# Second norm finished on VectorE and placed early in the step of a fused attention and mixture-of-experts layer

## The chip, the cores and the metric

One core of a Trainium2 chip runs the whole program. The metric is the device time in microseconds (us) of one execution. Three executions of the kernel before took 957.63, 956.96 and 951.90 us, median 956.96 us.

## The reference

For each of 8 batch rows of 1024 tokens with 256 features, the layer computes (cut to what matters; `mod` holds six vectors per row):

```
h = _layernorm(x) * (1 + ca) + sa
x = x + ga * _L0_attn_ref(h, W_in, W_out)   # Chebyshev features of q and k, 6 orders, 16 heads,
                                            # cumulative sums of k*v over the tokens, num / den
h = _layernorm(x) * (1 + cb) + sb           # the second norm
shared = silu(h @ sW1 + sb1) @ sW2 + sb2
activation = sqrt(softplus(h @ routing_W + bias)); the best 2 of 8 experts weigh
routed = sum_e cf[e] * (silu(h @ rW1[e] + rb1[e]) @ rW2[e] + rb2[e])
x = x + gb * (shared + routed)
```

All is float32. The second norm divides by sqrt(variance + 1e-5), over the 256 features of a token.

## The kernel before, in words

**Tiling.** A row is cut into two chunks of 512 tokens, p = 0 and p = 1. The program is a software pipeline over the 16 chunks. In the step (i, p) four chunks are worked on at once: chunk c+2 gets its first norm (ScalarE), chunk c+1 its q, k and v products, chunk c its attention, chunk c-1 its second norm, logits and routing weights, and chunk c-2 its nine experts (one shared, eight routed). The order of instructions on each engine is written out by hand in five functions `step`, one for each of TensorE, VectorE, ScalarE, GpSimd and the DMA queue of SyncE. Engines run their own lists strictly in order and meet only at semaphores. Steps (0,0) and (0,1) leave out what has no chunk yet, the last four leave out what has none any more; (7,1) has attention, second norm and experts, (8,0) second norm and experts, (8,1) experts alone.

**A step of TensorE (`step`, L1503).** Products of expert 0 and 1 into two PSUM banks that take turns (`ring`, L1368), the biases of the experts (L1476), transposes of the first norm (L1359), expert 0's second product (L1487), four of the six products for q and k, expert 1, transposes of the second norm, expert 2, the logits (L1394), sums over heads (L1421) with the transposed logits (L1402) between them, expert 3, v, expert 4, denominators (L1434), experts 5 to 8, then the projection `project_out` (L1445), which waits for VectorE's quotient `divide` (L1088), and last `combine_by_expert` (L1457, L1459), the transposes of the routing weights. A ring bank is filled again only once ScalarE has copied it out.

**The second norm before.** VectorE adds the projection to x (`residual`, L1096) and takes `bn_stats` (L378). GpSimd then works out mean and inverse deviation in ten small operations (`inv_std`, L353 to L366), and behind them in the same queue comes `weigh_order_5` (L653), a product of 128x1024 that VectorE's fifth prefix sum needs much later. ScalarE normalises the four token tiles (`normalise_second`, L435) in turn with its copies of q and k out of the ring (L800). TensorE transposes them, ScalarE scales the high parts (`highs`, L788), and VectorE makes the low parts (`lows(1)`, L968).

**The routing weights before.** `logit_parts` (L1107 to L1124), `exps` on GpSimd (L672), `softplus` (L1133 to L1150), `scores` on GpSimd (L681), `combine_weights` (L1158, L1162), seven small operations of `split_weights` on GpSimd (L698 to L703), `combine_by_expert` on TensorE, `combine_rows` on ScalarE (L860, L861), then DMAs that spread the rows over all partitions (`cfw`) for `weigh_hidden` (L1169), which VectorE does once for each of the eight experts.

**The quotient.** `invert` (L1072, L1074) on VectorE, a DMA to `inv_rows`, two that spread it back (L576, L581), `finish_numerator` (L1081), then `divide` (L1088). `output` (L1178) and two operations of `odd` for the next chunk (L984, L986) follow, and then `residual` of the next step.

## Time and profile before

| what | us |
|---|---|
| median of three executions | 956.96 |
| the profiled execution | 953.07 |
| its span, from first to last instruction | 951.3 |
| TensorE busy | 860.2 (90%) |
| VectorE busy | 815.7 (86%) |
| ScalarE busy | 489.8 (51%) |
| GpSimd busy | 408.3 (43%) |

The profiled execution lies 1.75 us above its span and 3.89 us below the median. Busy time of TensorE is that of pipelined matmuls and says nothing of how full the array is. In the middle of the program a row of the timeline is one instruction or a merged run of equal ones; what stands in brackets is the idle time of the engine before it and what ended that.

### The profile page before, as it was taken

The page shows a single profiled execution, that of the slowest core. Times are in us where ns is not written, and L with a number is a line of the kernel's source. Part 1 is how long each engine was busy: PE and PEld are TensorE (multiplying, and loading weights), DVE is VectorE, ACT ScalarE, POOL GpSimd, SP SyncE. Part 2 cuts the span into 40 slices and gives each one's busy share as a digit, 9 for nine tenths or more (in the row PEclk, how much of TensorE's full clock was granted, in tenths as well). Part 3 has the DMA queues.
Part 4 walks back from the last instruction along what each step waited for, and adds up shares of the span by engine and source line. Part 5 has one row for each costly group of instructions (what it writes and reads, how often), then busy time and mean ns, then how long its engine had stood idle before and what let it go on. Part 6 is the DMA issues. An engine that isn't in the chain of part 4 may idle for free. (4 is left out here: it accounts for less than half of the span.)

```text
span 951.3 us, 14272 instructions
## 1 busy us (share of the span) xinstructions
PE 860.2 (90%) x4377; PEld 648.6 (68%) x4377; DVE 815.7 (86%) x1263; ACT 489.8 (51%) x860; POOL 408.3 (43%) x502
## 2 busy tenths in 40 slices
PE   5766739999999999999999999999999999979998
PEld 4545427676767676786767676777767676756786
DVE  2696979999989998999989998999999998889423
ACT  4634546555556656655656566566556563441321
POOL 2341444363636355453636254543646253463220
PEclk9975769999999999999999999999999999999999
DMA  8014134453533535453534445354634243443422
GB/s 309 1 29 89 45 68 145 86 153 76 137 92 77 153 79 160 86 155 70 153 77 96 130 87 165 68 155 90 162 71 133 66 100 113 78 133 83 117 79 55
DMA packets 51705, 100.34 MB, mean 105 GB/s; under 512 B 5380, under 2 KB 34127, under 8 KB 49623
## 3 DMA queue, kind: packets, MB, share of 16 engines
q1 hardware_dynamic: 36356, 66.14, 21.2%
q0 software_dynamic: 14832, 33.03, 20.2%
q10 hardware_dynamic: 482, 0.74, 0.2%
q8 instruction: 18, 0.29, 0.1%
q14 instruction: 17, 0.13, 0.0%
HBM read 57.68 MB, written 17.06 MB: 79 GB/s over the span
## 5 line engine op out<-in xcount | busy, mean ns | idle before, releaser
L1487 PE MATMUL acc<-w,hid 128*128 128x256 f32 x1128 | 262.5, 380 | 2.6 <-DVE hid L1169 2.6
L1487 PEld LDWEIGHTS acc<-w,hid 128*128 128x128 f32 x1128 | 213.9, 190 | 37.6 <-DVE hid L1169 4.7
L845 ACT ACTIVATE hid<-ring,b1row 128x512 f32<-128x512 f32 x144 | 98.7, 685 | 143.0 <-PE ring L1368 140.4
L1169 DVE TENSOR_TENSOR hid<-hid,cfw 128x512 f32<-128x512 f32 x128 | 111.1, 870 | 37.0 <-DMA cfw<-cf_rows 21.6
L665 POOL DMA_DIRECT2D feat<-feat x48 | 43.7, 910 | 228.8 <-DVE feat L1046 115.0
L800 ACT ACTIVATE feat<-ring,bqkv 128x512 f32<-128x512 f32 x96 | 65.7, 686 | 81.9 <-PE ring L1368 81.9
L1368 PE MATMUL ring<-n2H,w1H 128*128 128x512 f32 x288 | 102.5, 437 | 0.0
L1445 PE MATMUL tr<-wo_g,feat 128*128 128x256 f32 x256 | 65.3, 413 | 35.9 <-DVE feat L1088 35.9
L1021 DVE TENSOR_TENSOR_SCAN feat<-zero,carry,feat 128x512 f32<-128x512 f32 x80 | 97.1, 1261 | 0.0
L1021 DVE TENSOR_TENSOR_SCAN feat<-zero,feat 128x512 f32<-128x512 f32 x80 | 95.7, 1243 | 0.0
L1368 PE MATMUL ring<-n2H,w1L 128*128 128x512 f32 x288 | 90.8, 397 | 0.0
L1368 PE MATMUL ring<-n2L,w1H 128*128 128x512 f32 x288 | 90.5, 395 | 0.0
L1421 PE MATMUL tr<-feat,const 128*32 128x512 f32 x640 | 89.1, 602 | 0.0
L1445 PEld LDWEIGHTS tr<-wo_g,feat 128*128 128x128 f32 x256 | 51.6, 207 | 49.2 <-DVE feat L1088 33.7
L1368 PE MATMUL ring<-n1H,winH 128*128 128x512 f32 x192 | 69.5, 444 | 15.2 <-issue 7.9
L820 ACT ACTIVATE feat<-feat,const 128x1024 f32<-128x1024 f32 x64 | 70.2, 1142 | 1.0
L353 POOL TENSOR_TENSOR ms<-stats 128x4 f32<-128x4 f32 x18 | 30.2, 1678 | 88.4 <-DVE stats L378 88.4
L1368 PEld LDWEIGHTS ring<-n2H,w1L 128*128 128x128 f32 x288 | 54.4, 189 | 12.7
L1368 PEld LDWEIGHTS ring<-n2L,w1H 128*128 128x128 f32 x288 | 54.5, 189 | 12.5
L1368 PE MATMUL ring<-n1H,winL 128*128 128x512 f32 x192 | 62.8, 409 | 0.0
L1368 PE MATMUL ring<-n1L,winH 128*128 128x512 f32 x192 | 62.8, 409 | 0.0
L1368 PEld LDWEIGHTS ring<-n2H,w1H 128*128 128x128 f32 x288 | 48.8, 191 | 18.5 <-issue 11.7
(171 smaller groups left out, 1559.8 us busy)
## 6 DMA issues: line engine op xcount, KB each, us to landing
feat<-feat POOLq DMA_DIRECT2D x48, 512.0 KB, 4.6
cfw<-cf_rows SPq DMA_DIRECT2D x16, 1280.0 KB, 7.6
xin<-in_L_attn_x SPq DMA_DIRECT2D x16, 512.0 KB, 9.3
feat<-inv_rows SPq DMA_DIRECT2D x32, 256.0 KB
cfw<-cf_rows SPq DMA_DIRECT2D x16, 512.0 KB, 3.6
out<-x SPq DMA_DIRECT2D x15, 512.0 KB, 8.5
out<-fin POOLq DMA_DIRECT2D x15, 512.0 KB, 6.0
cfw<-cf_rows SPq DMA_DIRECT2D x16, 256.0 KB, 4.5
```

The lines of the kernel that those rows point to most:

```text
L353: nc.gpsimd.tensor_tensor(t(1), m0, m1, ALU.subtract).then_inc(mv_steps[n], 1)
L665: g.dma_start(f(into), f(of), accum_op=ALU.add).then_inc(added[n], 16)
L800: a.activation(feat[:, (K0 + p, Q0 + p, V0)[m // 2], m % 2], ring[bank][:, :], ACT.Identity, bias=col(bqkv[:, (2, 3, 0, 1, 4, 5)[m]], i)). ...
L820: a.activation(f((qa, qb)[which - 1]), f(s), ACT.Square, bias=cv["biases"][:, which - 1:which]).then_inc(squares, 1)
L845: a.activation(hid[:, e % NG], ring[bank][:, :], ACT.Silu, bias=b1row[:, e:e + 1]).then_inc(ring_copied, 1)
L1021: last = v.tensor_tensor_scan(feat[:, W + n, h], zero[:, 0:1].to_broadcast([P, CT]), feat[:, W + n, h], carry[:, n, h:h + 1] if p else 0.0 ...
L1169: v.tensor_tensor(hid[:, e % NG], hid[:, e % NG], cfw[:, (e - 1) % NW], ALU.mult).then_inc(hidw_ready, 1)
L1368: last = mm(out, w, x, start=(n == 0), stop=(n == len(terms) - 1))
L1421: last = mm(tr[q][g_ * QS:(g_ + 1) * QS, :], cv["headsum"][:, (r // HPH) * QS:(r // HPH + 1) * QS], feat[:, srcs[n], h], start=(n < 4 and ...
L1445: last = mm(tr[t // 2][:, (t % 2) * D:(t % 2 + 1) * D], attn[:, k, t * P:(t + 1) * P], wo_g[:, k], start=(k == 0), stop=(k == KD - 1))
L1487: last = mm(acc[t // 2][:, t % 2], hid[:, e % NG, t * P:(t + 1) * P], w2[:, e], start=False, stop=(e == E), skip_group_check=True)
```

## The change

Two things are changed together. First, the arithmetic of the second norm: VectorE aggregates its own `bn_stats` with four `bn_aggr` and makes the variance plus epsilon and the negated mean with two `tensor_scalar` (`second_mean_var`); GpSimd keeps two operations, the power and one product (`second_inv_std`). `weigh_order_5` follows right behind them. Second, the order on every engine: the second norm is normalised in one piece before silu 1, its transposes stand on TensorE before the q and k products, its low parts on VectorE before the first prefix sum; softplus and the routing weights move forward; the transposes of the routing weights stand before the projection; on ScalarE `combine_rows` stands before the first norm of chunk c+2; on GpSimd the variance of that first norm stands behind `split_weights`; on SyncE the gate of the next row is loaded a step earlier.

```diff
+        def second_mean_var(dve, i, p):
+            c = number(i, p)
+            dve.wait_ge(stats_ready[1], c + 1)
+            dve.sem_inc(aggregate_begun, 1)
+            for t in range(NT):
+                last = nc.vector.bn_aggr(mean_var[:, t], stats[:, 1, t])
+            last.then_inc(aggregated, 1)
+            dve.wait_ge(aggregated, c + 1)
+            nc.vector.tensor_scalar(ms[:, 1, 8], mean_var[:, :, 1], EPS_LN, None, ALU.add).then_inc(mean_var_ready, 1)
+            nc.vector.tensor_scalar(ms[:, 1, 10], mean_var[:, :, 0], -1.0, None, ALU.mult).then_inc(mean_var_ready, 1)
+
+        def second_inv_std(pool, i, p):
+            c = number(i, p)
+            pool.wait_ge(mean_var_ready, 2 * c + 2)
+            ge(pool, norm_ready[1], c)
+            nc.gpsimd.tensor_tensor(ms[:, 1, 9], ms[:, 1, 8], k_("-half", NT), ALU.pow).then_inc(second_pow, 1)
+            pool.wait_ge(second_pow, c + 1)
+            nc.gpsimd.tensor_tensor(ms[:, 1, 11], ms[:, 1, 10], ms[:, 1, 9], ALU.mult).then_inc(rstd_ready[1], 1)
...
 # SyncE
-                    if loads or i < B:
-                        ge(sp, wo_ready, i)
-                        load_gate(i, 0)
+                    if i == 0:
+                        load_gate(0, 0)
...
+                if p == CB - 1 and i + 1 < B:
+                    sp.wait_ge(wo_ready, i + 1)
+                    load_gate(i + 1, 0)
...
 # GpSimd
-                    inv_std(pool, 1, *later(i, p, -1))
+                    second_inv_std(pool, *later(i, p, -1))
...
-                if st["attn"]:
-                    add_orders(i, p, 1)
-                if st["norm"]:
-                    inv_std_of_squares(pool, *later(i, p, 2))
                 if st["second"]:
                     exps(*later(i, p, -1))
                 if st["attn"]:
+                    add_orders(i, p, 1)
+                if st["second"]:
+                    scores(*later(i, p, -1))
+                if st["attn"]:
                     add_orders(i, p, 2)
                 if st["second"]:
-                    scores(*later(i, p, -1))
                     split_weights(*later(i, p, -1))
+                if st["norm"]:
+                    inv_std_of_squares(pool, *later(i, p, 2))
...
 # ScalarE
                 silu(0)
-                silu(1)
                 if qkv:
                     highs(0, *nxt)
+                if second:
+                    for t in range(NT):
+                        normalise_second(act, *prev, t)
+                silu(1)
                 silu(2)
                 if attn_:
                     scale_even(i, p)
-                for t, half in enumerate(HALVES[:4]):
-                    copy(half)
-                    if second:
-                        normalise_second(act, *prev, t)
-                silu(3)
                 if second:
                     highs(1, *prev)
-                silu(4)
+                for half in HALVES[:3]:
+                    copy(half)
                 if second:
                     copy_logits(*prev)
+                copy("q1")
+                silu(3)
+                silu(4)
...
                 silu(8)
+                if second:
+                    combine_rows(*prev)
                 if st["norm"]:
                     normalise_first(act, *later(i, p, 2))
...
 # VectorE
                     token_stats(dve, 1, *prev)
+                    second_mean_var(dve, *prev)
+                if qkv:
+                    lows(0, *nxt)
                 if attn_:
                     odd(i, p, 1)
                     weigh(i, p, 0)
-                if qkv:
-                    lows(0, *nxt)
+                    weigh(i, p, 1)
+                if second:
+                    lows(1, *prev)
                 if attn_:
-                    weigh(i, p, 1)
                     prefix(i, p, 0)
...
                 expert(5)
                 if second:
-                    softplus(*prev)
+                    combine_weights(*prev)
                 if attn_:
                     invert(i, p)
...
 # TensorE
                 if ffn:
                     expert_up(*exp, use, 0)
+                if qkv:
+                    transposes(0, *nxt)
+                if ffn:
                     expert_up(*exp, use, 1)
                     second_biases(*exp)
...
                 expert(0)
+                if second:
+                    transposes(1, *prev, behind_norm=qkv)
                 if qkv:
-                    for half in HALVES[:4]:
+                    for half in HALVES[:3]:
                         project(*nxt, use, half)
-                expert(1)
                 if second:
-                    transposes(1, *prev, behind_norm=qkv)
-                expert(2)
+                    route_logits(*prev)
+                if qkv:
+                    project(*nxt, use, "q1")
                 if second:
-                    route_logits(*prev)
+                    logits_by_token(*prev)
+                expert(1)
+                expert(2)
...
                 expert(8)
+                if second:
+                    combine_by_expert(*prev, attn_)
...
                     project_out(i, p)
-                if second:
-                    combine_by_expert(*prev, attn_)
```

The first place is VectorE from the residual to the first prefix sum of a step. `x<-tr,xin` is `residual`, `n1L` and `n2L` are `lows(0)` and `lows(1)`, `hid<-hid,cfw` weighs an expert, and the rows `feat<-feat` between are `odd` and `weigh`. Before:

```order
L378 BN_STATS stats<-x 128x6 [waits x1_ready,rstd1_ready]
L378 BN_STATS stats<-x 128x6 [waits x1_ready] x3
L984 SCALAR_TENSOR_TENSOR feat<-feat 128x1024 [waits squares]
L986 SCALAR_TENSOR_TENSOR feat<-feat 128x1024
L1002 TENSOR_TENSOR feat<-feat 128x1024
L968 SCALAR_TENSOR_TENSOR n1L<-tr,mods,n1H 128x512 [waits high0_ready] x2
L1004 SCALAR_TENSOR_TENSOR feat<-feat 128x1024 [waits projected]
```

and of the change:

```order
L381 BN_STATS stats<-x 128x6 [waits x1_ready,rstd1_ready]
L381 BN_STATS stats<-x 128x6 [waits x1_ready] x3
L390 BN_AGGR mean_var<-stats 128x2 [waits stats1_ready]
L390 BN_AGGR mean_var<-stats 128x2 x3
L393 TENSOR_SCALAR ms<-mean_var 128x4 [waits second_aggregated]
L394 TENSOR_SCALAR ms<-mean_var 128x4
L997 SCALAR_TENSOR_TENSOR n1L<-tr,mods,n1H 128x512 [waits high0_ready] x2
L1013 SCALAR_TENSOR_TENSOR feat<-feat 128x1024 [waits squares]
L1015 SCALAR_TENSOR_TENSOR feat<-feat 128x1024
L1031 TENSOR_TENSOR feat<-feat 128x1024
L1033 SCALAR_TENSOR_TENSOR feat<-feat 128x1024 [waits projected]
L997 SCALAR_TENSOR_TENSOR n2L<-tr,mods,n2H 128x512 [waits high1_ready] x2
```

Six small instructions and a wait come in, `lows(0)` moves ahead of four products of 128x1024, and `lows(1)` stands right behind them.

The second place is GpSimd at the start of the step of a new row, in the last rows. `wo_g<-wo,gates` is `scale_wo`. Of the change:

```order
L401 TENSOR_TENSOR ms<-ms,pool_c 128x4 [waits normalised1,second_mean_var]
L403 TENSOR_TENSOR ms<-ms 128x4 [waits second_pow]
L679 TENSOR_TENSOR feat<-feat 128x1024 [waits numerator,odd_ready]
L749 TENSOR_TENSOR wo_g<-wo,gates 128x512 [waits projected,ga_loaded]
L691 DMA feat<-feat 128x1024 [waits order_products]
```

Before, ten operations stood where two stand now, and the gate that `scale_wo` waits for was loaded in the same step.

The third place is ScalarE from the end of one step into the next. `cfT` and `cfR` are `combine_rows`, `ntok<-xin,ms` the first norm, `ntok<-x,ms` the second, `hid<-ring,b1row` a silu, `feat<-feat` the squares of q. Of the change:

```order
L887 ACTIVATE cfT<-misc 26x512 [waits combine_written]
L888 ACTIVATE cfR<-misc 50x512
...
L449 ACTIVATE ntok<-xin,ms 128x256 [waits rstd0_ready]
L449 ACTIVATE ntok<-xin,ms 128x256 x3
...
L844 ACTIVATE feat<-feat 128x1024 [waits order_products]
...
L847 ACTIVATE feat<-feat,const 128x1024 [waits squares] x2
...
L872 ACTIVATE hid<-ring,b1row 128x512 [waits ring_filled]
...
L815 ACTIVATE n1H<-tr,mods 128x512
...
L459 ACTIVATE ntok<-x,ms 128x256 [waits transposed1]
L459 ACTIVATE ntok<-x,ms 128x256 x3
```

Before, `combine_rows` was the last of these ahead of silu 0, behind the first norm and the squares.

## Rows read from the trace of the kernel before

**Rows 1.** Stretch, us, then busy PE, PEld, DVE, ACT, POOL (instructions); clock, DMA.
```profile
459.75:513.19 53.44, 51.16 (x268) 38.43 (x267) 50.02 (x80) 30.36 (x54) 26.49 (x30) 1.00 0.46 114
513.19:564.96 51.77, 50.79 (x268) 38.46 (x267) 50.04 (x77) 30.57 (x55) 24.46 (x30) 1.00 0.46 112
```

**Rows 2.** Waits: engine, line, releaser: us in total, times, longest.
```profile
PE tr L1445 <- DVE feat L1088: 35.9, 16, 12.2
```

**Rows 3.** Timeline of TensorE: start us, us, instruction, count, idle before.
```profile
473.55 0.73 PE L1368 MATMUL ring<-n1H,winH 128*128 128x512 f32 x2 [1.21 <-ACT feat L800]
...
509.78 3.72 PE L1445 MATMUL tr<-wo_g,feat 128*128 128x256 f32 x16 [1.08 <-DVE feat L1088]
```

**Rows 4.** Timeline of VectorE in both steps.
```profile
470.36 0.66 DVE L1169 TENSOR_TENSOR hid<-hid,cfw 128x512 f32<-128x512 f32 x1
...
472.42 2.67 DVE L1169 TENSOR_TENSOR hid<-hid,cfw 128x512 f32<-128x512 f32 x1 [0.26 <-DMA cfw<-cf_rows]
...
479.76 1.41 DVE L968 SCALAR_TENSOR_TENSOR n2L<-tr,mods,n2H 128x512 fp32r<-128x512 f32 x2 [2.22 <-ACT n2H L788]
...
493.31 0.37 DVE L1113 MAX8 top<-route 128x8 f32<-128x8 f32 x4
...
514.39 1.39 DVE L378 BATCH_NORM_STATS2 stats<-x 128x6 f32<-128x256 f32 x4
...
523.93 2.83 DVE L1169 TENSOR_TENSOR hid<-hid,cfw 128x512 f32<-128x512 f32 x1
...
531.65 0.75 DVE L968 SCALAR_TENSOR_TENSOR n2L<-tr,mods,n2H 128x512 fp32r<-128x512 f32 x1 [0.78 <-ACT n2H L788]
```

**Rows 5.** Timeline of VectorE around the quotient, p = 0 (two rows), then p = 1.
```profile
500.75 0.55 DVE L1074 RECIPROCAL denom<-denom 128x64 f32<-128x64 f32 x1
...
508.31 1.34 DVE L1088 TENSOR_TENSOR feat<-feat 128x512 f32<-128x512 f32 x2
...
552.46 0.55 DVE L1074 RECIPROCAL denom<-denom 128x64 f32<-128x64 f32 x1
...
558.16 0.29 DVE L1158 SCALAR_TENSOR_TENSOR route<-route,best 128x32 f32<-128x32 f32 x2
...
558.59 1.22 DVE L1081 TENSOR_TENSOR feat<-feat 128x1024 f32<-128x1024 f32 x1
560.18 1.34 DVE L1088 TENSOR_TENSOR feat<-feat 128x512 f32<-128x512 f32 x2 [0.37 <-DMA feat<-inv_rows]
```

**Rows 6.** Timeline of GpSimd in both steps.
```profile
466.99 3.17 POOL L363 TENSOR_TENSOR ms<-ms,pool_c 128x4 f32<-128x4 f32 x1
...
472.17 2.36 POOL L653 TENSOR_TENSOR feat<-feat 128x1024 f32<-128x1024 f32 x1
479.56 1.29 POOL L723 TENSOR_TENSOR wo_g<-wo,gates 128x512 f32<-128x512 f32 x1 [5.02 <-DMA gates<-gate_rows]
...
520.12 1.04 POOL L363 TENSOR_TENSOR ms<-ms,pool_c 128x4 f32<-128x4 f32 x1
...
522.78 3.42 POOL L653 TENSOR_TENSOR feat<-feat 128x1024 f32<-128x1024 f32 x1
```

**Rows 7.** Timeline of ScalarE, p = 0 and into the next step.
```profile
504.15 2.06 ACT L425 ACTIVATE ntok<-xin,ms 128x256 f32 x4
506.11 1.04 ACT L817 ACTIVATE feat<-feat 128x1024 f32<-128x1024 f32 x1
507.19 2.19 ACT L820 ACTIVATE feat<-feat,const 128x1024 f32<-128x1024 f32 x2
514.05 0.59 ACT L860 ACTIVATE cfT<-misc 26x512 f32<-26x512 f32 x1 [4.68 <-PE misc L1459]
```

**Rows 8.** Timeline of VectorE in the step (7,1).
```profile
849.38 1.50 DVE L968 SCALAR_TENSOR_TENSOR n2L<-tr,mods,n2H 128x512 fp32r<-128x512 f32 x2 [3.57 <-ACT n2H L788]
```

**Rows 9.** Timeline of TensorE in the step (8,0).
```profile
892.83 2.00 PE L1487 MATMUL acc<-w,hid 128*128 128x256 f32 x8 [0.82 <-DVE hid L1169]
...
900.51 0.66 PE L1402 MATMUL misc<-const,logT 128*128 128x128 f32 x4 [0.77 <-ACT logT L852]
```

37 lines of the change are left out of this document (15 added, 22 removed).

## The prediction, made before the changed kernel was timed

> **What bounds the kernel now.** I read the busy time of two whole steps first, then the waits, then the timelines of the same steps. In 53.44 us of a p = 0 step TensorE is busy 51.16 and VectorE 50.02; in 51.77 us of p = 1 they are busy 50.79 and 50.04 [rows 1]. So two engines are nearly full at once, and a gain on one alone is not worth its size. Which of them ends the step is seen where they meet: the projection waits for VectorE's quotient in every one of the 16 steps, 35.9 us in all [rows 2], 1.08 us at the end of the p = 0 step [rows 3]. Behind the quotient VectorE runs on into the next residual without a wait. VectorE sets the period, with TensorE about 1 us behind it. TensorE's other stall, 1.21 us at a ring bank [rows 3], is over before that wait and comes back as a longer or shorter wait there. It is worth nothing by itself.
>
> So I keep a ledger of what VectorE loses in a step beside its own work. **Before, p = 0:** 2.22 us waiting for the second norm's high parts, 0.26 for `cfw`, and 2.01 in a `weigh_hidden` that took 2.67 us where one of its kind takes 0.66 [rows 4]. GpSimd's fifth weighing ran from 472.17 for 2.36 us [rows 6], just across it. Sum 4.49. **Before, p = 1:** 0.78 us of waiting, 2.15 in the stretched `weigh_hidden` of 2.83 [rows 4], 0.37 for the spread inverse [rows 5]. Sum 3.30.
>
> **The change, part by part.**
>
> *Six small VectorE operations.* No row shows `bn_aggr`. Its nearest rows are four MAX8 in 0.37 us and four `bn_stats` over 256 elements in 1.39 us [rows 4]. It reads six elements, so I take the MAX8 end. With two short `tensor_scalar` (four MAX8 follow each other at 0.09 us) and a wait for its own semaphore I put the group at 0.7 us, bounds 0.6 and 1.7. `second_mean_var` then ends 3.3 us after the residual began (in p = 1: the statistics end at 515.78 [rows 4], 2.6 us after the step's start at 513.19 [rows 1], and 0.7).
>
> *GpSimd's chain.* Ten operations become two. The power takes 1.04 us when free and 3.17 us across VectorE's big products [rows 6]. Now VectorE stands in `lows(0)` or waits for it, so I take 1.04; with the product of 0.2 us and two hand-overs the inverse deviation is there at about 4.65 us. `weigh_order_5` follows for 2.36 us, until 7.0.
>
> *VectorE meets the weighing.* `lows(0)` (like `lows(1)` 1.4 us for both halves [rows 4]) is the only thing VectorE has ahead of `odd`, whose products are of the kind that collides with the weighing. Between 3.3 and 7.0 it does 1.35 us of work and loses 2.35. That is no less than the 2.0 to 2.15 it loses now: the weighing is hidden no better, only earlier. Whether `lows(0)` itself, with one input in PSUM, is held up by the weighing no row shows. The bounds are nothing, and the 2.15 us of a two-input product held behind it. I take nothing, because the first of the two halves is done before the weighing starts; the end of the range is 0.65, one half. The Trainium skill ("SBUF — State Buffer", section "Who interferes with whom") says that a VectorE instruction with at most one SBUF input does not contend with GpSimd, and one with two does, for the whole instruction. By it the term stays at nothing; by the bound the sum is 13 x 0.65 = 8.5 us longer.
>
> *`scale_wo`, p = 0 only.* Before, it ran for 1.29 us at 479.56 after waiting for its gate [rows 6], in the middle of VectorE's 2.22 us of idleness. It cost nothing. Now the gate has been loaded long before, so it stands right behind the weighing, among VectorE's two-input products. That cover is gone: 1.29 us.
>
> *`lows(1)` without a wait.* From 7.0 VectorE has four products, each 1.22 us by itself and some 1.15 behind another [rows 5], until 11.6. ScalarE: silu 0 and `highs(0)`, 2.06 us of normalising, two silus, `scale_even` of about 2 us, `highs(1)`. It has the first high half at about 11.6. The 2.22 and 0.78 us go, barely.
>
> *The quotient.* From the end of the reciprocal to `divide` there are 508.31 - 501.30 = 7.01 us in p = 0, without a wait, and 560.18 - 553.01 = 7.17 in p = 1, with 0.37 of waiting [rows 5]. `combine_weights` (558.16 to 558.59, 0.43) moves ahead of the reciprocal. The DMA chain stays at about 7.17, so the wait grows to 0.5 in p = 0 and 0.8 in p = 1. The 0.43 us is not saved.
>
> *Routing earlier.* `cfw` comes sooner: the 0.26 us goes. TensorE's transposes of the routing weights (some 0.4 us) now lie in its wait for the quotient, worth nothing while VectorE ends the step.
>
> **Ledger after.** p = 1: 0.7 + 2.35 + 0.8 = 3.85, against 3.30: +0.55. p = 0: 0.7 + 2.35 + 1.29 + 0.5 = 4.84, against 4.49: +0.35. Seven p = 0 steps (rows 1 to 7 of the batch) and six p = 1: 7 x 0.35 + 6 x 0.55 = 5.75 us.
>
> *The ends.* In (7,1) there is no `lows(0)`, so `odd` starts at once and the power is blocked for its 3.17 us. VectorE waits 3.57 us for high parts there now [rows 8], and the weighing lies in that wait. After, the chain power 3.17, product up to 1.2, normalising 2.06, silus 1.2, `scale_even` 2.0, one high half 0.7 is 10.3 us against 4.5 us of products. The wait stays or grows by up to 2, and the small operations (0.7) and the quotient (0.43) come on top: +1.1 to +3.3, taken 2.2. In (8,0) TensorE idles 0.82 + 0.77 us now [rows 9]. After, with no q and k products between, the logits wait about 2.3 us for the norm's low parts and the transposed logits 0.8 for ScalarE, less 0.4 of transposes moved out: +1.1. The first steps, where terms of both signs appear without experts, I put at nothing.
>
> Sum: 5.75 + 2.2 + 1.1 = 9.05 us on the profiled execution's 953.07 (3.89 below the median of 956.96): **962 us**.
>
> **A second loop, close behind.** ScalarE now holds `combine_rows`, 4.68 us of waiting for TensorE before [rows 7], ahead of the first norm and the squares. From TensorE's transposes on: 1.2 + 2.06 + 1.04 + 2.19 [rows 7] = 6.5, then silu, two high parts, the second norm, two silus, `scale_even`, two high parts and the first copy, 9.1 us, and hand-overs of 0.2. Only then can TensorE do q. From there to the next transposes it has 50.8 less 11.05 for what lies ahead and 3.6 for the projection, plus 0.4: 36.5. Loop: 52.3 us. VectorE's period by the ledger is 51.77 + 0.55 = 52.3 in p = 1 and 53.8 in p = 0. They are level, so any delay on ScalarE counts.
>
> **The rivals.**
>
> *Faster (0.15).* GpSimd does not get at the shared path while VectorE's products follow each other without a gap. If `lows(0)` ends before the weighing starts at 4.65, the weighing may be held off until `lows(1)`, beside which it runs, and costs about 1 us. Ledger: 0.7 + 1.0 + 0.8 = 2.5 in p = 1 (-0.8) and 3.5 in p = 0 (-1.0): -12 us, about 942. For it: the weighing of p = 1 was held for about 1 us (3.42 against 2.36 [rows 6]). Against it: it was let in after that, and VectorE then lost 2.15.
>
> *No difference (0.22).* The terms are tenths of a us on 13 steps; TensorE's absent ring stall and the earlier `cfw` leave less jitter. 949 to 957.
>
> *GpSimd's queue comes late (0.12).* The variance of the first norm now stands behind the seven operations of `split_weights`. Each of the eleven may wait for the end of a VectorE product of 1.13 us. Between reciprocal and quotient I count them done at 49.5 us after the residual, and ScalarE wants the result at 50.8. If each waits in full, 11 x 1.13 = 12.4 from 40.2 is 52.6: 1.8 late, and the ScalarE loop becomes 54.1 against an average of 52.6 now: 13 x 1.5 = 20 us, 973 to 980.
>
> *The new pieces are dear (0.09).* `bn_aggr` near its upper bound (+1.0 each step) or `lows(0)` held (+0.65): 970 to 975.
>
> My own case, 957 to 968, has 0.42. That leaves the range 948 to 976.
>
> A measurement can tell about 1% from no change. Of my case somewhat under half lies above 1%, and both dear rivals do. That gives faster 0.15, within 1% 0.47, slower 0.38.
>
> **What would show it.** In the timeline after: `bn_aggr` four in about 0.4 us; the power near 1.0 us with `lows(0)` beside it; the weighing right behind, and VectorE's first `odd` beginning as it ends, or stretched by 2 us; in p = 0 a second stretched product across `scale_wo`; `weigh_hidden` always near 0.67; no wait before `lows(1)`; a wait of 0.5 to 0.8 for the inverse; a ring stall of 1 to 1.5 us before q on TensorE. The prediction is wrong if the projection no longer waits for VectorE, or if the first norm on ScalarE waits for GpSimd, or if the power takes 3 us in most steps.

## The result, and the profile after

The changed kernel takes **994.1 us** (median of 4, 990.2 to 1003.5). The kernel before took 954.4 us on the same chip, so the ratio is **1.043, 95% interval [1.034, 1.052]**: slower, and 32 us above the forecast of 962, outside its range. The profiled execution spans 994.8 us against 951.3, at a mean clock of 0.951 against 0.964.

I cut both traces at the first residual of each step. Nearly all of the loss lies in the thirteen steps (1,0) to (7,0): 727.5 us now, 687.7 before, **39.8 us or 3.06 per step**. Step (7,1) adds 3.4 us, what follows it 0.8; the start is 0.4 us shorter. Three of the thirteen: the shortest p = 0 step, a long one and the p = 1 step behind that. Each row is a stretch, then busy PE, PEld, DVE, ACT, POOL, clock, DMA share and GB/s, as in [rows 1]:

```profile
254.26:308.84 54.58, 51.62 (x267) 38.20 (x266) 50.99 (x86) 29.75 (x56) 22.28 (x22) 1.00 0.44 113
...
474.90:532.78 57.88, 53.60 (x268) 39.38 (x267) 52.28 (x85) 30.52 (x56) 22.16 (x22) 0.97 0.43 106
532.78:588.24 55.46, 52.64 (x272) 39.21 (x271) 50.71 (x82) 29.47 (x54) 19.20 (x21) 1.00 0.42 99
```

A step lasts 54.2 to 58.0 us (51.7 to 54.3 before), and the four longest, 57.1 to 58.0 us, show a clock of 0.95 to 0.99. The totals of the waits (engine, line, releaser: us in total, times, longest), of TensorE and of VectorE, say where to look. The first answers to [rows 2]; the second was 10.0 us in 12 times before:

```profile
PE tr L1474 <- DVE feat L1117: 42.7, 16, 5.5
```

```profile
DVE feat L1117 <- DMA feat<-inv_rows: 37.6, 16, 3.8
```

VectorE's front part first, in the shortest p = 0 step (timeline: start us, us, instruction, count, idle before). It answers to [rows 4] and runs much as forecast:

```profile
257.01 0.38 DVE L390 BATCH_NORM_AGGREGATE mean_var<-stats 128x2 f32<-128x6 f32 x4 [0.15 <-DVE stats L381]
...
257.70 1.41 DVE L997 SCALAR_TENSOR_TENSOR n1L<-tr,mods,n1H 128x512 fp32r<-128x512 f32 x2
259.03 1.22 DVE L1013 SCALAR_TENSOR_TENSOR feat<-feat 128x1024 f32<-128x1024 f32 x1
260.16 3.39 DVE L1015 SCALAR_TENSOR_TENSOR feat<-feat 128x1024 f32<-128x1024 f32 x1
...
265.74 1.40 DVE L997 SCALAR_TENSOR_TENSOR n2L<-tr,mods,n2H 128x512 fp32r<-128x512 f32 x2
...
295.02 0.55 DVE L1103 RECIPROCAL denom<-denom 128x64 f32<-128x64 f32 x1
...
304.16 1.29 DVE L1117 TENSOR_TENSOR feat<-feat 128x512 f32<-128x512 f32 x2 [1.85 <-DMA feat<-inv_rows]
```

The small operations, `lows(0)`, a product stretched by 2.2 us, `lows(1)` without a wait: all there. What the forecast did not have is in the last row. The quotient now starts 8.6 us behind the end of the reciprocal (7.0 in [rows 5]) and waits 1.85 us. GpSimd in the same step, answering to [rows 6], shows what stands before it:

```profile
257.76 1.04 POOL L401 TENSOR_TENSOR ms<-ms,pool_c 128x4 f32<-128x4 f32 x1 [3.57 <-DVE ms L394]
...
259.05 3.41 POOL L679 TENSOR_TENSOR feat<-feat 128x1024 f32<-128x1024 f32 x1
265.48 1.49 POOL L749 TENSOR_TENSOR wo_g<-wo,gates 128x512 f32<-128x512 f32 x1 [3.02 <-DMA gates<-gate_rows]
...
288.80 0.92 POOL L691 DMA_DIRECT2D feat<-feat  x1 [8.27 <-DVE feat L1075]
...
292.32 1.98 POOL L707 TENSOR_TENSOR best<-best,pool_c 128x8 f32<-128x8 f32 x1 [2.60 <-DVE best L1179]
294.26 0.90 POOL L691 DMA_DIRECT2D feat<-feat  x1
```

L691 issues the accumulating DMAs of `add_orders`, L707 is `scores`. The second add is issued at 288.80. The third, which must wait for the second's landing, now stands behind `scores` too and is issued at 294.26, 5.5 us later. On SP's queue in that step come the write of the inverse to DRAM and its spread back over the partitions:

```profile
295.60 0.62 SPq L600 DMA_DIRECT2D inv_rows<-denom  x1
299.23 1.23 SPq L605 DMA_DIRECT2D feat<-inv_rows  x2
```

The spread waits until the write has landed: **3.6 us** from the issue of the one to the issue of the other. In the kernel before, the add preceded the write by 2.8 us (GpSimd, then SP), and the same distance is 2.0:

```profile
493.36 0.87 POOL L665 DMA_DIRECT2D feat<-feat  x1 [7.07 <-DVE feat L1046]
...
498.48 0.91 POOL L665 DMA_DIRECT2D feat<-feat  x1 [0.26 <-issue]
```

```profile
501.32 0.63 SPq L576 DMA_DIRECT2D inv_rows<-denom  x1
503.36 1.21 SPq L581 DMA_DIRECT2D feat<-inv_rows  x2
```

The third add came 5.1 us behind the second there, hardly sooner than now. What moved more is the write: 8.0 us behind the second add before, 6.8 now. `logit_parts`, 2.1 us of VectorE between the second add and the inverse, has gone forward, and only `combine_weights` (0.8 us with its wait) has come in.

TensorE waits for the quotient. The timeline at the end of the step that begins at 474.90, and stretches of it:

```profile
525.81 0.49 PE L1488 MATMUL misc<-const,split 128*64 128x128 f32 x3
528.83 5.40 PE L1474 MATMUL tr<-wo_g,feat 128*128 128x256 f32 x16 [2.53 <-DVE feat L1117]
```

```profile
526.00:529.00 3.00, 0.47 (x4) 0.21 (x3) 1.60 (x3) 2.55 (x5) 0.75 (x2) 1.00 0.08 27
529.00:533.00 4.00, 4.00 (x12) 3.21 (x13) 3.38 (x5) 3.73 (x5) 1.36 (x1) 0.58 0.89 232
```

After 2.5 us of idleness the granted clock is 0.58 for the projection (the lower of the two levels, 1.2 GHz, for most of it), and its 16 matmuls take 5.40 us instead of the 3.72 of [rows 3]. That happened at the end of five of the thirteen steps (5.36 to 6.71 us), and in the kernel before of one; otherwise the projection took 3.7 us. Over the whole span the same 256 matmuls are busy for 73.4 us, against 65.3:

```profile
L1474 PE MATMUL tr<-wo_g,feat 128*128 128x256 f32 x256 | 73.4, 450 | 42.7 <-DVE feat L1117 42.7
```

```profile
L1445 PE MATMUL tr<-wo_g,feat 128*128 128x256 f32 x256 | 65.3, 413 | 35.9 <-DVE feat L1088 35.9
```

**The 39.8 us, on VectorE.** VectorE goes from residual to residual, so its own time adds up to the steps. Between its quotient's and its next residual's start almost nothing changed (1.8 us more in all); from the end of the reciprocal to the quotient it is 21.2 us more, and the reciprocal ends 1.2 us later behind the residual in p = 0 and 1.4 in p = 1, 16.8 us in all. By kind, summed over the same thirteen steps, with what the forecast's ledger had for the same kind:

| VectorE, thirteen steps, us | before | changed | difference | forecast |
|---|---|---|---|---|
| waits for the spread inverse | 6.1 | 29.4 | +23.3 | +6.1 |
| waits for the projection, at the residual | 1.0 | 9.9 | +8.9 | none |
| waits for `scores`, at `combine_weights` | 0 | 4.6 | +4.6 | none |
| waits for high parts (of both norms) | 19.0 | 2.0 | -17.0 | -20.2 |
| waits for `cfw` | 3.2 | 0 | -3.2 | -1.8 |
| the six small operations and their wait | 0 | 9.7 | +9.7 | +9.1 |
| products, scans and `weigh_hidden`, stretched ones included | 463.0 | 473.0 | +10.0 | +12.6 |
| the rest | | | +3.5 | none |

7.3 of the 9.9 us at the residual lie behind slowed projections. On TensorE the same loss shows as 15.2 us more of waiting at the projection (31.4 against 16.1) and 8.0 us of longer projections.

### The profile page after: what moved, and what is told of

It is laid out like the page before. It is cut to its first block and busy times, and to the rows that moved or that the text cites. A ratio compares the mean times of both kernels' runs of the same rounds, so it can differ in the third digit from the quotient of the medians.

```text
span 994.8 us, 14220 instructions
## 1 busy us (share of the span) xinstructions
PE 875.2 (88%) x4377; PEld 650.4 (65%) x4377; DVE 836.9 (84%) x1359; ACT 483.3 (49%) x860; POOL 346.5 (35%) x374
## 5 line engine op out<-in xcount | busy, mean ns | idle before, releaser
L1516 PE MATMUL acc<-w,hid 128*128 128x256 f32 x1128 | 268.3, 383 | 8.3 <-DVE hid L1198 8.1
L1516 PEld LDWEIGHTS acc<-w,hid 128*128 128x128 f32 x1128 | 210.5, 189 | 54.5 <-DVE hid L1198 23.2
L872 ACT ACTIVATE hid<-ring,b1row 128x512 f32<-128x512 f32 x144 | 96.7, 682 | 197.5 <-PE ring L1397 197.5
L691 POOL DMA_DIRECT2D feat<-feat x48 | 43.9, 915 | 353.6 <-DVE feat L1071 219.7
L1198 DVE TENSOR_TENSOR hid<-hid,cfw 128x512 f32<-128x512 f32 x128 | 86.4, 677 | 30.7 <-ACT hid L872 21.3
L1474 PE MATMUL tr<-wo_g,feat 128*128 128x256 f32 x256 | 73.4, 450 | 42.7 <-DVE feat L1117 42.7
L1397 PE MATMUL ring<-n2H,w1H 128*128 128x512 f32 x288 | 108.1, 456 | 0.0
L1474 PEld LDWEIGHTS tr<-wo_g,feat 128*128 128x128 f32 x256 | 57.2, 229 | 56.7 <-DVE feat L1117 34.5
L1450 PE MATMUL tr<-feat,const 128*32 128x512 f32 x640 | 85.5, 596 | 0.0
L1397 PEld LDWEIGHTS ring<-n2L,w1H 128*128 128x128 f32 x288 | 54.3, 189 | 12.9
L1075 DVE SCALAR_TENSOR_TENSOR feat<-feat 128x1024 f32<-128x1024 f32 x48 | 58.8, 1225 | 2.8 <-DVE carry L1059 2.0
```

Source lines behind the costliest of these rows:

```text
L691: g.dma_start(f(into), f(of), accum_op=ALU.add).then_inc(added[n], 16)
L872: a.activation(hid[:, e % NG], ring[bank][:, :], ACT.Silu, bias=b1row[:, e:e + 1]).then_inc(ring_copied, 1)
L1075: v.scalar_tensor_tensor(out=w, in0=w, scalar=GAMMA[n], in1=f((Q0 + p, 0, QT3, 0, QT5)[n]), op0=ALU.mult, op1=ALU.mult).then_inc(products, 1)
L1198: v.tensor_tensor(hid[:, e % NG], hid[:, e % NG], cfw[:, (e - 1) % NW], ALU.mult).then_inc(hidw_ready, 1)
L1397: last = mm(out, w, x, start=(n == 0), stop=(n == len(terms) - 1))
L1450: last = mm(tr[q][g_ * QS:(g_ + 1) * QS, :], cv["headsum"][:, (r // HPH) * QS:(r // HPH + 1) * QS], feat[:, srcs[n], h], start=(n < 4 and ...
```

## Experiments

Two theories stood against each other: **T1**, the third add in the way of the inverse; **T2**, the order of the rest, above all the early weighing and the waits for high parts. In the diffs, - is the kernel named first.

**The third add left out** (the output then lacks the third order's sum, and `finish_numerator` waits for the first two adds instead of the third), from the changed kernel:

```
-                if st["attn"]:
-                    add_orders(i, p, 2)
```

> The changed kernel without the third accumulating DMA (the sum of orders is left incomplete, so that part of the computation is missing). Theory 1: write to spread near 2.0 us in every step and reciprocal to quotient 7 us or less, steps of 52 to 53 us, total 950 to 960. Theory 2: both stay at 3.6 and 9.0 us, total about 990.

One execution: 960.7 us. Write to spread 2.0 us in every step, quotient 6.9 to 7.9 behind the reciprocal. T1's direction, but a DMA left out says nothing on what its place alone is worth.

**Orders early.** GpSimd's queue goes add, add, exps, add, scores, as in the kernel before (add, exps, add, scores, add in the changed one), and VectorE's `logit_parts` goes back behind order product 3:

```
+                if st["attn"]:
+                    add_orders(i, p, 1)
                 if st["second"]:
                     exps(*later(i, p, -1))
                 if st["attn"]:
-                    add_orders(i, p, 1)
+                    add_orders(i, p, 2)
                 if st["second"]:
                     scores(*later(i, p, -1))
-                if st["attn"]:
-                    add_orders(i, p, 2)
-                if st["second"]:
                     split_weights(*later(i, p, -1))
...
                 expert(3)
-                if second:
-                    logit_parts(*prev)
...
                     order_product(i, p, 2)
                     order_product(i, p, 3)
+                if second:
+                    logit_parts(*prev)
```

> The changed kernel with the GpSimd order of before for the three accumulating DMAs (second one ahead of exps, third ahead of scores) and logit_parts back behind the fourth order product. Theory 1 (the third accumulating DMA, issued 1.3 us before the inverse's write instead of 2.8, shares the DMA engines with the write and its spread): the third DMA comes at about 37 us of the step, write to spread falls from 3.6 to about 2.1 us, reciprocal to quotient from 9.0 to about 7.3, TensorE's wait for the projection back to 1 to 1.5 us, the low-clock steps vanish, total 955 to 962. Theory 2 (the quotient is late for another reason, ScalarE or SyncE's own queue): reciprocal to quotient stays near 9, total within 5 us of 994.

979.4 us, ratio to before 1.023 [1.019, 1.028]. The add is 4.3 us ahead of the write, write to spread 2.0, middle steps at clock 1.00. That takes 15 of the 40 us away: T1 is true and not the whole. Two moves make the distance of 4.3 us, and the larger is `logit_parts` (see the table of the adds below). The new order also costs something: the third waits for the landing of the second, and `scores` stands behind it, so VectorE waits more at `combine_weights`, which the change put ahead of the inverse (7.6 us in the changed kernel):

```profile
DVE route L1186 <- POOL best L707: 17.9, 16, 1.8
```

**The reverse, in the kernel before:** `scores` ahead of the third add, nothing else.

```
+                if st["second"]:
+                    scores(*later(i, p, -1))
                 if st["attn"]:
                     add_orders(i, p, 2)
                 if st["second"]:
-                    scores(*later(i, p, -1))
                     split_weights(*later(i, p, -1))
```

> The kernel before with one change: scores ahead of the third accumulating DMA on GpSimd, so that this DMA is issued about 3.5 us later, just behind the inverse's write. Theory 1: write to spread or reciprocal to quotient grows by 1 to 2 us, TensorE's wait for the projection to 2 to 3 us with stretches of lower clock, total 975 to 990. Theory 2: the third DMA was not awaited, so the total stays within 3 us of the kernel before.

1020.6 us, ratio **1.066 [1.062, 1.069]**, worse than I expected. The add comes 1.0 us *behind* the write, so the write is quick and the spread is caught instead. The add also lands so late that `finish_numerator`, which needs it, waits (VectorE in one step, then TensorE):

```profile
425.75 1.25 DVE L1082 TENSOR_TENSOR feat<-feat 128x1024 f32<-128x1024 f32 x1 [0.79 <-DMA feat<-feat]
429.31 1.29 DVE L1089 TENSOR_TENSOR feat<-feat 128x512 f32<-128x512 f32 x2 [2.30 <-DMA feat<-inv_rows]
```

```profile
430.73 5.40 PE L1446 MATMUL tr<-wo_g,feat 128*128 128x256 f32 x16 [4.15 <-DVE feat L1089]
```

Over the thirteen steps VectorE waits 30.3 us for the spread and 10.2 for the add itself. One swap of two GpSimd instructions costs 64 us here, and the two ways in which it does are not told apart by a run.

**The add ahead of scores alone**, and `combine_weights` behind expert 6, from the changed kernel:

```
+                if st["attn"]:
+                    add_orders(i, p, 2)
                 if st["second"]:
                     scores(*later(i, p, -1))
-                if st["attn"]:
-                    add_orders(i, p, 2)
```

> The changed kernel with two moves taken back on GpSimd's way to the inverse: the third accumulating DMA goes ahead of scores, and combine_weights, which waits for scores, goes behind expert 6. Nothing else of the order is undone. Theory 1 (the third add, issued 1.3 us before the write of the inverse, delays the write and the spread): the add is then issued about 2.4 us before the write, from the write to the spread 2.0 to 2.4 us instead of 3.6, the quotient 7 to 8 us behind the reciprocal instead of 8.6 to 9.6, steps of 52.5 to 54.5 us, no step at a clock below 0.98 but the first and last: 965 to 978 us. Rival (the length comes from the rest of the new order, whatever the DMA does): from the write to the spread falls, and the time stays at 985 to 995, because TensorE waits elsewhere.

984.5 us, 1.028 [1.024, 1.032]. My expectation of 2.4 us was wrong: the add is issued 0.6 us ahead and write to spread is 4.2. Each add waits for the landing of the one before, so the third cannot come sooner than 5.1 us behind the second, which waits for a product of VectorE. With `combine_weights` out of its way the inverse comes sooner still:

```profile
506.36 0.91 POOL L691 DMA_DIRECT2D feat<-feat  x1 [8.27 <-DVE feat L1075]
511.51 0.85 POOL L691 DMA_DIRECT2D feat<-feat  x1 [4.24 <-DMA feat<-feat]
```

And yet VectorE waits only 10.4 us for the inverse in the whole run, against 37.6: what holds this kernel is something else, which its totals of waits show (7.6 and 7.9 in the changed kernel):

```profile
DVE route L1187 <- POOL best L707: 25.6, 15, 2.6
DVE n1L L997 <- ACT n1H L815: 32.0, 15, 4.7
```

`scores` now stands behind the third add and so behind the second's landing. `combine_weights` waits for it, `split_weights` and the first norm's variance come late behind that on GpSimd, ScalarE's first norm waits for the variance (0.59 us at 524.13), and VectorE for the high parts. So this run says little on the price of write to spread. It shows which path holds the step next.

**The inverse early**, from the changed kernel:

```
+                expert(5)
                 if second:
                     softplus(*prev)
+                if attn_:
+                    invert(i, p)
                 if qkv:
                     clip(*nxt, use, 0)
                     clip(*nxt, use, 1)
-                expert(5)
                 if second:
                     combine_weights(*prev)
-                if attn_:
-                    invert(i, p)
```

> The changed kernel with invert moved ahead on VectorE: behind the denominator products come expert 5, softplus, invert, clips, combine_weights. Theory 1 (the DMA chain behind the reciprocal, now 8.6 to 9.3 us, sets the quotient, VectorE idles in it): the reciprocal ends about 1.6 to 1.9 us earlier in the step (39.3 instead of 41.3), the idle before the quotient shrinks by as much or the step does, total 965 to 975. Theory 2 (VectorE's own work sets the step): the wait for the inverse goes, and the total falls by less than 5 us.

976.4 us, 1.022 [1.018, 1.026]. The inverse is written 1.06 us ahead of the add, write to spread 2.0, and the quotient still comes 9.0 to 10.1 us behind the reciprocal, which is 2 to 3 us earlier.

**ScalarE's order of before**, from the changed kernel: `combine_rows` last, and on GpSimd the first norm's variance ahead of exps.

```
+                if st["norm"]:
+                    inv_std_of_squares(pool, *later(i, p, 2))
                 if st["second"]:
                     exps(*later(i, p, -1))
```

> The changed kernel with combine_rows last on ScalarE again (behind the first norm and the squares) and the first norm's variance on GpSimd back ahead of exps. Theory 3 (the new ScalarE order delays silu 0 and the high parts of the next step and so VectorE's low parts): the idle before lows(0) of 0 to 1 us and the 1 us before the second norm fall, ScalarE's 5 to 6 us of waiting for the routing transposes is filled; but while the DMA chain sets the quotient the total falls only by 0 to 8 us, and the write still takes 3.6 us to the spread. If Theory 1 covered everything, no change beyond 3 us.

1004.8 us, 1.055 [1.049, 1.060]: a miss. Nor was there much for it to mend: in the changed kernel VectorE waits for high parts only 2.0 us in the thirteen steps. The four operations of the variance go ahead of `exps` and push the adds back again; in p = 1 the third stands 0.6 us ahead of the write, write to spread 4.3. Two moves are mixed here, and no run has ScalarE's alone.

These runs together show how the first part works. Over the eighteen kernels that have the add, by how far its issue precedes the write's (typical steps):

| add ahead of the write, us | write to spread, us | kernel |
|---|---|---|
| 4.27 | 2.00 | orders early |
| 2.84 | 2.05 | before, p = 0 |
| 2.72 | 2.19 | before, p = 1 |
| 1.34 | 3.60 | changed |
| 0.64 | 4.3 | add ahead of scores |
| -0.03 | 2.06 | three mended (below) |
| -1.00 | 1.97 | scores first, in before |

Between 0.2 and 2.9 us the two columns add up to 4.85 to 5.03 us in 154 of 158 steps (5.3 to 7.0 in the other four): **the spread is issued some 4.93 us after the add, however late the write between them was issued.** The add's own landing says why: in the thirteen steps of the changed kernel it is recorded 4.69 to 4.75 us behind the add's issue, and the spread is issued 0.23 or 0.24 us after it each time. The Trainium skill ("DMA: Bandwidth & Descriptors", section "Queues, rings and completion order") says that a transfer's semaphore increment lands only after every earlier write of the same DMA engine, across its queues. The trace agrees with its 0.23 us, the free write of a negative distance included; no run isolates the increment from the data.

Where the distance comes from, p = 0 steps, medians:

| kernel | second to third add, us | second add to write, us |
|---|---|---|
| before | 5.12 | 7.97 |
| changed | 5.46 | 6.79 |
| orders early | 5.11 | 9.51 |
| add ahead of scores | 5.16 | 5.91 |
| scores first, in before | 8.95 | 7.96 |

5.1 us is the second add's time to landing and its hand-over. In the changed kernel, standing behind `scores` costs the third add only 0.3 us of the 1.5 us of distance that were lost; 1.2 us come from the inverse's being written sooner behind the second add. In the kernel before, the same place behind `scores` costs 3.8 us, since softplus, which `scores` waits for, stands right ahead of the inverse there.

**The arithmetic alone**: the kernel before with bn_aggr, the two small operations and the two-operation `second_inv_std`, at their old places.

```
-                    inv_std(pool, 1, *later(i, p, -1))
+                    second_inv_std(pool, *later(i, p, -1))
...
                     token_stats(dve, 1, *prev)
+                    second_mean_var(dve, *prev)
```

> The kernel before, order untouched, with the second norm's arithmetic alone changed (bn_aggr and two small operations on VectorE, two left on GpSimd). Theory A (the arithmetic is cheap, the new order is what costs): VectorE plus 0.7 us a step, the wait for the second norm's high parts shrinks by about as much or more in p = 0, total within 6 us of the kernel before, 950 to 963. Theory B (the arithmetic itself costs, by the small operations or by the weighing falling elsewhere): plus 1 us a step or more, 968 or above.

951.1 us, 0.9965 [0.9944, 0.9986]: not slower at all. The loss comes with the order. Here the weighing runs beside `lows(0)`, which stands behind three products, and costs VectorE 0.87 us instead of 2.17.

**Three and four repairs at once.** Orders early, ScalarE's order of before and the inverse ahead of softplus (with `combine_weights` behind expert 6); then also the gate loaded at the start of the p = 1 step and `scale_wo` ahead of the power; then also the two `lows` later. The inverse's move, the same in all three:

```
+                expert(5)
+                if attn_:
+                    invert(i, p)
                 if second:
                     softplus(*prev)
...
-                expert(5)
```

> The changed kernel with three things mended: logit_parts and the GpSimd order of the accumulating DMAs as before, ScalarE's combine_rows and the first norm's variance as before, and invert right behind expert 5, ahead of softplus. If the terms found so far (DMA chain, scores waiting behind the third DMA 0.96, ScalarE late 1.0 us) are all there is, VectorE idles nowhere over 0.3 us, steps take 51.5 to 52.5 (p = 1) and 52.5 to 53.5 us (p = 0), total 945 to 958. If something else sets the step, it stays above 965.

> As c1_three_mended, with the gate of the next row loaded at the start of the step p = 1 and scale_wo ahead of the second norm's power on GpSimd, where VectorE reads PSUM or one SBUF input. Theory: the 1.0 us by which scale_wo stretches a prefix sum in every p = 0 step goes, 7 us less than c1_three_mended. Rival: scale_wo delays the power and with it the norm by its 1.3 us, equal or slower than c1_three_mended.

> The kernel with all four moves (orders early, ScalarE's order of before, inverse behind expert 5, gate loaded first), in which in addition lows(0) stands behind odd, and lows(1) behind the first prefix. There GpSimd's fifth weighing should run across lows(0), which has one input in PSUM, and no longer across odd. Theory 2 (what is left of the loss is VectorE's product stretched by 2.17 us across the weighing, because the early order leaves it no cover): the stretched product shrinks from 3.38 us to about 2.1, steps from 53.75 and 53.9 to 52.3 to 52.9, time 953 to 962 us against 973.8. Rival (the stretch is paid wherever the weighing stands; or TensorE, which waits 2.0 to 2.3 us for weighed experts now, waits more for the later low parts): steps stay at 53.5 to 54.3, 970 to 978 us.

976.6 (1.024 [1.019, 1.029]), 973.8 (1.021 [1.017, 1.026]) and 978.9 us (1.022 [1.018, 1.026]). The quotient waits for no DMA in any of them, and yet every step takes about 54 us. VectorE and TensorE now wait for each other elsewhere. One of my repairs was itself a fault, as the next pair suggests.

**In the kernel with the arithmetic alone: lows(1) one product later**, then **the inverse ahead of softplus** as well.

```
+                if attn_:
+                    order_product(i, p, 0)
                 if second:
                     lows(1, *prev)
                 if attn_:
-                    order_product(i, p, 0)
                     order_product(i, p, 1)
```

> The kernel before with the new arithmetic of the second norm and the old order, and lows(1) one product later (behind order_product 0, 1.22 us). VectorE's wait of 1.6 us for the high parts is then filled by a product. Theory (VectorE sets the period of the old order): steps 52.3 and 53.3 become 51.5 to 52.3, 938 to 946 us. Rival (TensorE, busy 51.2 us of each step, is as near: the logits wait for the low parts, or its ring stalls instead): 948 to 952, no change.

> The one before this, and the inverse straight behind expert 5, ahead of softplus and the clips. The chain of small DMAs then starts 2 to 3 us earlier and TensorE's wait of 1.0 to 1.9 us for the quotient goes, if the third accumulating DMA, now issued only about 0.5 us before the write, does not take it back. Theory: write to spread grows to 3.5 to 4.4 us as in the other kernel with both moves, the quotient still comes without a wait, steps 51.3 to 52.0: 932 to 942 us. Rival (the third add at 0.5 us before the write costs more than the 2.3 us that the inverse is early): as long as the one before this, or longer, 945 to 965.

The first of the two: **937.8 us, 0.979 [0.975, 0.984]**, better than both kernels. VectorE's wait of 1.6 us before `lows(1)` is mostly filled by a product of about 1.2 (VectorE):

```profile
523.02 1.19 DVE L1069 SCALAR_TENSOR_TENSOR feat<-feat 128x1024 f32<-128x1024 f32 x1
524.73 1.41 DVE L991 SCALAR_TENSOR_TENSOR n2L<-tr,mods,n2H 128x512 fp32r<-128x512 f32 x2 [0.52 <-ACT n2H L811]
```

The second: 968.0 us, 30 us worse by one move (expert 5 goes ahead of the clips with it). The inverse now asks for TensorE's denominators before they are there, and the experts behind it come late (waits of VectorE, then of TensorE):

```profile
DVE denom L1095 <- PE misc L1459: 30.7, 15, 2.7
```

```profile
PE acc L1512 <- DVE hid L1192: 25.9, 16, 4.6
```

The three kernels with this move wait for the denominators too (14.4 to 46.5 us in all), so they say nothing on T2, which was tried again without it.

**Both lows later, from the kernel with orders early**: `lows(0)` behind odd, `lows(1)` behind the first prefix.

```
+                if attn_:
+                    odd(i, p, 1)
                 if qkv:
                     lows(0, *nxt)
                 if attn_:
-                    odd(i, p, 1)
                     weigh(i, p, 0)
                     weigh(i, p, 1)
+                    prefix(i, p, 0)
                 if second:
                     lows(1, *prev)
-                if attn_:
-                    prefix(i, p, 0)
```

> The changed kernel with the orders early (979.4 us), in which lows(0) stands behind odd, and lows(1) behind the first prefix; the inverse stays where the change put it. Theory 2 (the early weighing has no PSUM operation of VectorE beside it, and VectorE waits for the high parts of the first norm): the product stretched to 3.38 us shrinks to about 2.1, the wait of 0.8 to 1.1 us before lows(0) goes, steps from 53.3-54.1 and 54.6-56.1 to 52.0-53.0 and 53.0-54.5: 955 to 966 us. Rival (TensorE is the bound, as the later low parts hold the projections and the logits): 974 to 985.

955.8 us, 0.999 [0.996, 1.002]: **23.6 us less by two moves on VectorE**, T2 as expected. VectorE and GpSimd now, in the step from 459.93:

```profile
465.50 1.40 DVE L996 SCALAR_TENSOR_TENSOR n1L<-tr,mods,n1H 128x512 fp32r<-128x512 f32 x2
466.82 2.23 DVE L1030 TENSOR_TENSOR feat<-feat 128x1024 f32<-128x1024 f32 x1
```

```profile
465.60 2.37 POOL L679 TENSOR_TENSOR feat<-feat 128x1024 f32<-128x1024 f32 x1
```

The weighing runs beside `lows(0)`, which takes its usual 1.40 us, and only its tail meets a product. In the thirteen steps the products take 9.8 us less and VectorE waits 6.5 less for the first norm's high parts, out of 21.3. What is left is the wait for `scores`, 12.4 us, which the kernel before does not have; no run moves `combine_weights` back alone.

**The first of the two moves alone**, and **both moves with the third add left late**:

> The changed kernel with the orders early (979.4 us) and lows(0) alone behind odd; lows(1) stays behind weigh 1. Then the weighing runs across lows(0) and the wait of 0.8 to 1.1 us before it goes, but the norm on ScalarE starts 0.9 us later, and VectorE may wait about 1 us before lows(1). If the first move carries it: 955 to 963 us. If VectorE then waits for the second high parts as much as it gained: 966 to 976.

> The changed kernel with lows(0) behind odd and lows(1) behind the first prefix, and nothing else: the third accumulating DMA stays 1.3 us ahead of the write. If the two causes add up, 994 less 23.6 is 970 us, from the write to the spread 3.6 us as before, steps of 53 to 54.5 us. Rival (VectorE's gain only lengthens its wait for the spread inverse, and the DMA chain holds the step): 980 to 990.

974.0 us, 1.020 [1.016, 1.024]: the first move is worth 5.4 us, since VectorE then waits some 1.3 us a step before `lows(1)`; the second brings the other 18.2. And 974.8 us, 1.021 [1.018, 1.024]: from 994.1 the two moves bring 19.3 us with the add late and 23.6 with it early; the early adds bring 14.7 without the moves and 19.0 with them. The two causes nearly add up.

**The gate and scale_wo early**, on top of orders and lows:

> The one before this, and the gate loaded at the start of the p = 1 step and scale_wo ahead of the second norm's power. It then runs beside the residual and the statistics, which read PSUM or one input, and not beside a scan of VectorE. Theory: the scan that takes 3.38 us in p = 0 goes back to 2.33, p = 0 steps 0.5 to 1.0 us shorter, 3 to 7 us in all. Rival (VectorE does not set the p = 0 step then): within 2 us of the kernel before this one.

950.6 us, 0.992 [0.990, 0.995]: 5.2 us. `scale_wo` leaves the neighbourhood of the two-input operations and runs beside the residual. With the early norm so mended, the kernel is a little faster than before.

**lows(1) later in the kernel before**, its ten GpSimd operations untouched:

> The kernel before, with its ten operations of the second norm on GpSimd, and lows(1) behind the first order product: the move that brought the new arithmetic in the old order from 951.1 to 937.8 us. Theory (the move fills VectorE's wait for high parts, whatever made it): in p = 0 the wait of 2.22 us shrinks by 1.2, in p = 1 that of 0.78 goes, ten to thirteen us less, 942 to 947; with the weigh_hidden of 2.67 us still stretched. Rival (without the new arithmetic the high parts come so late that VectorE waits again elsewhere): 950 to 958.

942.3 us, 0.985 [0.981, 0.988]. So of the best version's 2.1%, 1.5% are this one move, and the new arithmetic adds about half a per cent.

## Why the prediction was wrong, point by point

- **The step that failed: "The DMA chain stays at about 7.17, so the wait grows to 0.5 / 0.8".** The quotient came 8.6 to 9.6 us behind the reciprocal, and VectorE's wait for the spread inverse was 1.9 to 2.7 us instead of 0.5 and 0.8. I counted what VectorE does between reciprocal and quotient and did not follow GpSimd's queue to its third add. The diff takes `logit_parts` out from between the second add and the inverse, which brings the write 1.2 us nearer, and puts the third add behind `scores`, 0.3 us. The row was in the trace: issued 2.84 us ahead of the write, it stood almost exactly at the 4.93 - 2.0 = 2.9 us from which it does no harm, so any smaller distance had to cost. The wait grew by 23.3 us, forecast 6.1.
- **The clock was no term at all.** A wait of 1.1 us at the projection leaves it at full speed; behind waits of 2.1 to 2.9 it fell in five of the thirteen steps. The projections took 8.0 us longer than before, and VectorE waited 7.3 us behind slowed ones at the residual. In the kernel before, the steps from (1,0) to (6,1) with waits of 1.0 to 1.7 stay at 1.00.
- **`combine_weights` ahead of the inverse** was counted as work of 0.43 us. Its wait for `scores` was no term: 4.6 us, and 12 to 13 once the adds are early.
- **The rest of VectorE's ledger held**: stretched operations +10.0 us (forecast +12.6), high parts -17.0 (forecast -20.2). I had the stretched product of 2.2 us right (3.39 against 1.22) and called it "hidden no better, only earlier". T2's repairs bring 19 to 24 us all the same: a place beside `lows(0)` was free. So that gain is not a loss which the forecast missed, but one that the change could have avoided.
- **bn_aggr and the small operations**: 3.4 us behind the residual, forecast 3.3. The power took 1.04 us, as taken. Right; the arithmetic alone even gains 0.35%.
- **lows(0) beside the weighing**: no cost, 1.40 us in 465.50 above. The sentence of the Trainium skill ("SBUF — State Buffer", section "Who interferes with whom") holds, that a VectorE instruction with at most one SBUF input does not contend with GpSimd, and so does its other half, on two inputs: such products beside the weighing took 2.08 to 3.40 us instead of 1.22.
- **scale_wo, 1.29 us**: about right. In the step shown it waited 3.02 us for its gate, ran at 265.48 beside `lows(1)` and cost nothing. In the other six p = 0 steps it ran across a product of VectorE, which then took 2.30 to 2.32 us for 1.22, 1.1 us each (below, VectorE and GpSimd). It cost in the repaired kernels too: with orders early it ran across a scan (3.38 us for 2.33) in p = 0, and with the `lows` later it stretched a `weigh_hidden` to 1.3 to 1.7. Loading the gate and running `scale_wo` early took 5.2 us off, 0.7 per p = 0 step.

```profile
485.13 2.32 DVE L1031 TENSOR_TENSOR feat<-feat 128x1024 f32<-128x1024 f32 x1
```

```profile
484.99 1.38 POOL L749 TENSOR_TENSOR wo_g<-wo,gates 128x512 f32<-128x512 f32 x1 [0.87 <-DMA gates<-gate_rows]
```

- **(7,1)**: +3.4, forecast +2.2 (up to 3.3). **(8,0) and the tail**: +0.8, forecast +1.1. Right in size.
- **The second loop on ScalarE**: not binding in the changed kernel, where VectorE waits 2.0 us for high parts in the thirteen steps. It does bind once the adds go ahead of `scores`: 25.9 us of waiting for the first norm's high parts with the third add and `combine_weights` moved, 6.5 with the orders early. The rival of GpSimd's queue (0.12) named the right queue and, for the changed kernel, the wrong victim: it priced the variance, and what was late was a DMA. Its 973 to 980 fell short as well.

I gave slower 0.38 and within 1% 0.47. The error was not the chance of a rival but a missing rival. What stays open: why the clock falls in some steps with a wait of 2.1 or 2.2 us and not in one with 2.8, and what the wait for `scores` would be worth if `combine_weights` alone went back behind the inverse.

## What to carry to other kernels

When instructions change places on an engine that issues DMAs, or on one whose work those DMAs wait for, write down for each DMA what it is issued behind, before and after, and which small latency-bound transfer on another queue comes within its time in flight; here that distance set the price, and an order change on VectorE moved it more than the one on GpSimd. Put GpSimd's large product beside a VectorE operation that reads PSUM, and give a late input one more product of cover rather than an earlier place. Test one move at a time: three repairs together hid a move that cost 30 us by itself in another kernel. And when a repair gives less than expected, read the totals of waits again: another path may have become the longest.

## What the runs showed of the hardware

- Behind a 512 KB accumulating DMA, the small write of the inverse lets the spread be issued 4.93 us after that DMA's issue, for distances from 0.2 to 2.9 us (154 of 158 steps); behind none, or ahead of it, 2.0 us after its own. With the write ahead by 1.0 us, the spread is held instead, and in the kernel with `scores` first the quotient comes at 10.0 us, not 7.0, part of it by waiting for the add itself.
- Four `bn_aggr` of six elements take 0.38 us, 0.09 apart; the 128x4 power takes 1.04 us with `lows(0)` beside it and 1.91 to 2.01 where `odd` stands there (as in the kernel with the arithmetic alone).
- In the step at 474.90, after 2.5 us without a matmul, the clock was granted at 0.58 in the 4 us that followed, and 16 matmuls took 5.40 us for 3.72. After 2.81 us in another step it stayed at 1.00.
